# Graph layer and LayerNorm: one pass over column halves in eight banks, with A^T turned by VectorE

## The chip, the cores and the metric

One Trainium2 chip, one of its cores. The metric is the device time of one execution in microseconds. TensorE (PE) multiplies into PSUM, VectorE (DVE) and ScalarE (ACT) do the elementwise work, GpSimd (POOL) a little, and SyncE (SP) issues every DMA. PSUM has eight banks of 128 x 512 float32, and a matmul here fills one bank's width.

## What is computed

With x of 2048 x 512 and A = `adj` of 2048 x 2048, both float32:

```python
S = (A + A.T) * 0.5 + I
deg = S.sum(axis=1); dinv = deg ** -0.5            # 0 where deg <= 0
y = A @ (dinv[:, None] * S * dinv[None, :])        # Coefficient2 is adj, too
y = y @ x
out = layernorm(x + y)                             # over the 512 columns
```

Both kernels compute it as two products: U = dinv * (S @ (dinv * x)) and then A @ U. A matmul here takes the operand that is held in the array ("weights") transposed, so product 2 needs tiles of A^T in SBUF, and product 1 uses that S is symmetric. Each float32 operand is split into a high part (rounded to `float32r`) and a low part (what is left), and each product of two tiles is three matmuls: high with high, high with low, low with high.

## The kernel before

The matrices are cut into 16 blocks of 128 rows (N = 2048, NB = 16).

*Transposes.* Strip j is rows 128j to 128j+127 of A (`strip_row`, ring of 4), and `strip_col` holds the column block j below the diagonal. `transpose_batch` turns them on TensorE, 128 x 128 at a time, four to a batch, into banks 6 and 7; ACT copies each batch into `AT` (L342, `copy_batch`). There are 136 such transposes of row strips and 120 of column blocks, 256 in all.

*Degrees.* `row_sums` (DVE, L457) adds A^T's strip to A's strip in place and sums along the row; `sums_to_degrees`, `degree_root` (ACT, L356), `invert_root` (DVE, L493) and `degree` give dinv of the strip.

*Product 1.* The 16 row blocks of U are made in three groups of 6, 5 and 5 banks (`GROUPS`), and each group runs over all 16 strips k. For group 0, MH and ML are the high and low part of the first 768 columns of M = A + A^T in the strip (ACT L377, DVE L442) and ZH and ZL those of dinv * x (ACT L346, DVE L447). The strips' transposes run between group 0's products. Groups 1 and 2 load 640 columns of each strip again into `natural`, add A^T (L521), and split again. The "+ I" of S is worked in by `ex_scale` on POOL and `finish_u` on DVE (L515), which also release the banks between the groups.

*Product 2.* For each of the 16 output blocks m and each half h of the contraction (8 blocks), `half_high` (ACT, L412) and `half_low` (DVE, L539) split 128 x 1024 of `AT` into ATH and ATL, double-buffered; `column` runs 24 matmuls on each half. `layer_norm` follows a block behind.

Engines take their instructions in program order and wait on semaphores. `contract` on TensorE starts a step when both low parts are there:

```python
pe.wait_ge(ml_done, s + 1)
pe.wait_ge(zl_done, s + 1)
```

Of the kernel before, what the change touches and what calls it, by code (L numbers as in the profile page):

```python
# [5 lines left out]
P = 128  # L26
# [6 lines left out]
DEG_MIN = 1e-34  # L33
RING_R = 4
BATCH = 4
PIECES = 4


def gnn_resnorm_kernel(nc: bass.Bass, x: bass.AP, adj: bass.AP, out: bass.AP):
    N, D = x.shape  # L40
    NB = N // P
    GROUPS = [range(0, 6), range(6, 11), range(11, 16)]
    assert N == 2048 and D == 512 and GROUPS[-1][-1] == NB - 1
    GW = len(GROUPS[0]) * P
    G1 = len(GROUPS[1])
    UX_STEP = NB // 2
    HALF = NB // 2

    def batches(j):
        rows = [("row", c, min(BATCH, NB - c)) for c in range(j, NB, BATCH)]
        cols = [("col", r, min(BATCH, NB - r)) for r in range(j + 1, NB, BATCH)]
        return rows + cols

    BATCHES = [batches(j) for j in range(NB)]
    BATCH_BASE = [sum(len(b) for b in BATCHES[:j]) for j in range(NB + 1)]


    STRIPS = [[2], [3], [4, 5]] + [[j + 3] if j + 3 < NB else [] for j in range(3, NB)]  # L60
# [3 lines left out]
    AHEAD = 4  # L64
    FIRST_ROUND = [0, 0, 0, 2, 2]

    COPIES_FOR_SUM = [4, 2, 4, 3, 0]
    COPIES_FOR_D = [1, 2, 0, 2, 2, 0]

    def between_products(j):  # L70
        return [(i, n) for i in STRIPS[j] for n in range(len(BATCHES[i]))] 

    with ExitStack() as ctx:


        top = [(nc.sbuf_base + 31) // 32 * 32]
# [4 lines left out]
        def sb(name, shape, dt):  # L81
            size = 4
            for n in shape:
                size *= n
            top[0] += (size + 31) // 32 * 32
            return at(name, shape, dt, top[0] - (size + 31) // 32 * 32)

        AT = sb("AT", [NB, N], F32)
        uh_at = top[0]
        UH = sb("UH", [NB, D], F32R)  # L90
        ul_at = top[0]
        UL = sb("UL", [NB, D], F32R)
        strip_row = at("strip_row", [RING_R, N], F32, uh_at)
        ux = at("ux", [NB, D], F32, ul_at)
        strip_col = at("strip_col", [2, NB - 1, P], F32, ul_at + 8 * D * 4)

        slots_at = top[0]
        SLOT = 2 * D + 2 * GW
        sb("slots", [2, SLOT], F32)

        def in_slot(name, shape, dt, skip):
            return [at(f"{name}{i}", shape, dt, slots_at + (i * SLOT + skip) * 4) for i in range(2)]

        ZH = in_slot("ZH", [D], F32R, 0)
        ZL = in_slot("ZL", [D], F32R, D)
        MH = in_slot("MH", [GW], F32R, 2 * D)
        ML = in_slot("ML", [GW], F32R, 2 * D + GW)
        ATH = in_slot("ATH", [HALF, P], F32R, 0)
        ATL = in_slot("ATL", [HALF, P], F32R, HALF * P)

        xr = sb("xr", [2, D], F32)
        outr = sb("outr", [2, D], F32)
        natural = [at("natural0", [G1 * P], F32, top[0] - 2 * D * 4),
                   at("natural1", [G1 * P], F32, uh_at + 13 * D * 4)]
        ident = sb("ident", [P], F32)

# [27 lines left out]

        piece_in = [sem(f"piece_in{i}") for i in range(2 * PIECES)]
        row_in = [sem(f"row_in{i}") for i in range(RING_R)]
        col_in = [sem(f"col_in{i}") for i in range(2)]
        nat_in = [sem(f"nat_in{i}") for i in range(2)]
        x_in = [sem(f"x_in{i}") for i in range(2)]
        ux_in = [sem(f"ux_in{i}") for i in range(3)]  # L150
# [4 lines left out]
        msum_done = sem("msum_done")  # L155
        partial_done = sem("partial_done")
        PIECEWISE = 4
        PARTS = [sum(sum(kind == "col" for kind, _, _ in b) for b in BATCHES[:j]) for j in range(PIECEWISE + 1)]
        deg_done = sem("deg_done")
        newton_chain = sem("newton_chain")  # L160
        half_ready = sem("half_ready")
        degc_ready = sem("degc_ready")
        root_done = sem("root_done")
        inv_done = sem("inv_done")
        dinv_ready = sem("dinv_ready")
        mh_done = sem("mh_done")
        ml_done = sem("ml_done")
# [3 lines left out]
        ex_done = sem("ex_done")  # L171
        u_done = sem("u_done")
# [11 lines left out]
        LAST1 = 3 * NB  # L184

        def row_nth(j):
            return 16 * (j // RING_R + (j % RING_R > 0))

        def col_nth(j):
            return 16 * ((j + 1) // 2)  # L190

        def nth(s, slot):
            return 8 * s + (16 - 8 * slot)

        WIDTHS = [len(g) for g in GROUPS]
# [8 lines left out]
        def degree(j, engine, scaled):
            c = slice(j, j + 1)
            engine.wait_ge(inv_done, j + 1)
            scaled(corr[:, c], inv[:, c], deg_neg[:, c], 0.0).then_inc(newton_chain, 1)
            engine.wait_ge(newton_chain, 3 * j + 1)  # L210
            scaled(corr2[:, c], corr[:, c], inv[:, c], 1.5).then_inc(newton_chain, 1)
            engine.wait_ge(newton_chain, 3 * j + 2)
            scaled(dinv_open[:, c], corr2[:, c], inv[:, c], 0.0).then_inc(newton_chain, 1)
            engine.wait_ge(newton_chain, 3 * j + 3)
            scaled(dinv[:, c], dinv_open[:, c], mask[:, c], 0.0).then_inc(dinv_ready, 1)
            engine.wait_ge(dinv_ready, j + 1)
            scaled(dinv_half[:, c], dinv[:, c], 0.5, 0.0).then_inc(half_ready, 1)
# [8 lines left out]
        def _(sp):  # L226
            def load_x(k, s, slot):
                sp.dma_start(xr[:, slot, :], block(x, k)).then_inc(x_in[slot], 16)  # L228

            def load_ux(g, blocks):  # L230
                for m in blocks:
                    sp.dma_start(ux[:, m, :], block(x, m)).then_inc(ux_in[g], 16)  # L232

            def load_rows(j):
                if j >= RING_R:
                    sp.wait_ge(ml_done, j - RING_R + 1)
                if j == 0:
                    for n in range(PIECES):
                        cols = slice(n * N // PIECES, (n + 1) * N // PIECES)
                        sp.dma_start(strip_row[:, 0, cols], block(adj, 0)[:, cols]).then_inc(piece_in[n], 16)  # L240
                else:
                    sp.dma_start(strip_row[:, j % RING_R, :], block(adj, j)).then_inc(row_in[j % RING_R], 16)

            def load_cols(j):
                if j >= 2:
                    sp.wait_ge(tr_copied, BATCH_BASE[j - 1])
                size = BATCH if j == 0 else NB
                for n, r in enumerate(range(j + 1, NB, size)):
                    last = min(r + size, NB)
                    sp.dma_start(strip_col[:, j % 2, r - j - 1:last - j - 1, :],  # L250
                                 adj[r * P:last * P, j * P:(j + 1) * P].rearrange("(r p) c -> p r c", p=P)
                                 ).then_inc(col_in[j % 2] if j else piece_in[PIECES + n], 16)

            for j in range(RING_R):
                load_rows(j)
                if j < 3:
                    load_cols(j)
                if j < 2:
                    load_x(j, j, j)
            load_rows(RING_R)  # L260
            load_cols(3)
            for j in range(2, NB):
                if 2 < j < NB - 2:
                    load_rows(j + 2)
                sp.wait_ge(zl_done, j - 1)
                load_x(j, j, j % 2)
                if 1 < j and j + 2 < NB - 1:
                    load_cols(j + 2)
# [421 lines left out]
```

## Time and profile before

| | |
|---|---|
| time, median of 3 runs (lowest, highest) | 414.69 us (414.6, 416.33) |
| span of the profiled execution | 413.7 us |
| PE busy, share of span, instructions | 390.5 us, 94%, 1792 |
| DVE busy | 255.9 us, 62% |
| ACT busy | 166.6 us, 40% |
| DMA | 60.47 MB, mean 146 GB/s |
| first product matmul starts | 21.79 us |
| product 2 starts; last matmul starts | 233.20 us; 407.22 us |

The span runs from the first to the last instruction of one profiled execution. The timed runs lie about 1.0 us above it. A matmul's busy time in the trace overlaps its neighbours', so its pace is read from the starts of consecutive matmuls.

### The profile page before, as it was taken

The numbers are of one execution on the slowest core, as the hardware profiler recorded it, in microseconds if no ns is written. First come the engines' busy times: TensorE is split into PE (matmuls) and PEld (weight loads), VectorE is DVE, ScalarE is ACT, GpSimd is POOL, SyncE is SP. The second block draws the span as 40 slices with busy tenths as digits, with TensorE's granted clock in tenths as the row PEclk, the third lists the DMA queues.
The fourth block names the chain that finished last, engine by engine and source line by source line (L and its number), as shares of the span: only waits on it lengthen the run. The fifth ranks groups of instructions, "written<-read, shape, count | busy, mean of one in ns | idle before, by whom it ended". The sixth has DMA issues, their size and how long they took to land.

```text
span 413.7 us, 5648 instructions
## 1 busy us (share of the span) xinstructions
PE 390.5 (94%) x1792; PEld 318.8 (77%) x1792; DVE 255.9 (62%) x499; ACT 166.6 (40%) x309; POOL 50.5 (12%) x38
## 2 busy tenths in 40 slices
PE   5899999999988999979999999999999999999994
PEld 4677788777766888858888888888888888888883
DVE  0496877888798666897666654444455555554442
ACT  4666788676653444443344522222211222222210
POOL 0000000430079000094000430000000000000000
PEclk9999999999999999989999999999999999999998
DMA  7997988974474656766667001111111111111111
GB/s 229 353 345 242 361 272 278 398 291 155 117 248 131 178 176 173 206 199 165 175 175 189 26 2 51 52 51 51 51 51 51 51 51 51 48 35 42 28 49 51
DMA packets 36829, 60.47 MB, mean 146 GB/s; under 512 B 2640, under 2 KB 18000, under 8 KB 34896
## 3 DMA queue, kind: packets, MB, share of 16 engines
q1 hardware_dynamic: 36816, 60.30, 46.2%
q8 instruction: 7, 0.11, 0.1%
q14 instruction: 6, 0.05, 0.0%
HBM read 56.10 MB, written 4.19 MB: 146 GB/s over the span
## 4 chain that ended last, share of the span: by engine, by line
PE 78%; DVE 9%; DMA 5%; SPq 3%; ACT 2%; issue 2%; DVEq 0%; ACTq 0%
PE bank L609 25%; PE bank L611 24%; PE bank L610 24%; PE bank L605 5%; DMA strip_row<-in_adj 4%; DVE strip_row L457 2%; DVE ML L442 2%; DVE ZL L447 1%; DVE ux L515 1%; ACT AT L342 1%; SPq L232 1%; DMA natural<-in_adj 1%; ACT ZH L346 1%; SPq L228 1%; SPq L250 1%
## 5 line engine op out<-in xcount | busy, mean ns | idle before, releaser
L609 PE MATMUL bank<-ZL,MH 128*128 128x512 f32 x256 | 105.0, 410 | 7.9 <-DVE ML L442 6.1
L611 PE MATMUL bank<-ZH,MH 128*128 128x512 f32 x256 | 100.7, 393 | 0.0
L610 PE MATMUL bank<-ZH,ML 128*128 128x512 f32 x256 | 100.4, 392 | 0.0
L609 PE MATMUL bank<-UL,ATH 128*128 128x512 f32 x256 | 99.7, 389 | 0.0
L610 PE MATMUL bank<-UH,ATL 128*128 128x512 f32 x256 | 99.6, 389 | 0.0
L611 PE MATMUL bank<-UH,ATH 128*128 128x512 f32 x256 | 99.6, 389 | 0.0
L539 DVE TENSOR_TENSOR ATL<-AT,ATH 128x1024 fp32r<-128x1024 f32 x32 | 40.3, 1259 | 77.7 <-ACT ATH L412 77.7
L412 ACT ACTIVATE ATH<-AT 128x1024 fp32r (+1 forms) x32 | 34.0, 1061 | 84.1 <-PE bank L611 84.1
L609 PEld LDWEIGHTS bank<-ZL,MH 128*128 128x128 f32 x256 | 48.5, 190 | 19.5 <-DVE ML L442 9.1
L346 ACT ACTIVATE ZH<-xr,dinv 128x512 fp32r<-128x512 f32 x48 | 34.5, 719 | 59.4 <-DMA xr<-in_x 30.2
L611 PEld LDWEIGHTS bank<-ZH,MH 128*128 128x128 f32 x256 | 48.3, 189 | 10.4
L609 PEld LDWEIGHTS bank<-UL,ATH 128*128 128x128 f32 x256 | 48.0, 188 | 10.3 <-DVE ATL L539 0.3
L611 PEld LDWEIGHTS bank<-UH,ATH 128*128 128x128 f32 x256 | 48.1, 188 | 10.1
L610 PEld LDWEIGHTS bank<-UH,ATL 128*128 128x128 f32 x256 | 48.1, 188 | 9.8
L610 PEld LDWEIGHTS bank<-ZH,ML 128*128 128x128 f32 x256 | 48.7, 190 | 8.3
L447 DVE SCALAR_TENSOR_TENSOR ZL<-xr,dinv,ZH 128x512 fp32r<-128x512 f32 x48 | 40.3, 839 | 21.7 <-ACT ZH L346 21.6
L457 DVE SCALAR_TENSOR_TENSOR strip_row<-strip_row,AT 128x2048 f32<-128x2048 f32 (+8 forms) x27 | 38.1, 1431 | 19.6 <-ACT AT L342 19.6
L342 ACT ACTIVATE AT<-bank 128x512 f32<-128x512 f32 (+3 forms) x76 | 38.8, 527 | 27.6 <-PE bank L605 27.5
L326 POOL TENSOR_TENSOR UL<-ux,UH 128x512 fp32r<-128x512 f32 x16 | 25.6, 1631 | 113.5 <-ACT UH L352 113.5
L316 POOL TENSOR_SCALAR ux<-ux,dinv 128x512 f32<-128x512 f32 x16 | 24.2, 1530 | 76.2 <-DMA ux<-in_x 76.2
L521 DVE TENSOR_TENSOR natural<-natural,AT 128x640 f32<-128x640 f32 x32 | 27.1, 846 | 8.8 <-DMA natural<-in_adj 8.4
L605 PE MATMUL bank<-ident,strip_row 128*128 128x128 f32 x136 | 23.8, 309 | 7.6 <-DMA strip_row<-in_adj 6.9
(46 smaller groups left out, 250.8 us busy)
## 6 DMA issues: line engine op xcount, KB each, us to landing
xr<-in_x SPq DMA_DIRECT2D x64, 256.0 KB, 3.5
strip_row<-in_adj SPq DMA_DIRECT2D x15, 1024.0 KB, 7.3
natural<-in_adj SPq DMA_DIRECT2D x32, 320.0 KB, 3.4
ux<-in_x SPq DMA_DIRECT2D x16, 256.0 KB, 5.1
out<-outr SPq DMA_DIRECT2D x16, 256.0 KB, 2.0
strip_row<-in_adj SPq DMA_DIRECT2D x4, 256.0 KB, 4.3
strip_col<-in_adj SPq DMA_DIRECT2D x4, 256.0 KB, 6.8
strip_col<-in_adj SPq DMA_DIRECT2D x1, 896.0 KB, 9.6
```

What stands on the lines that cost most here:

```text
L326: nc.gpsimd.tensor_tensor(UL[:, m, :], ux[:, m, :], UH[:, m, :].bitcast(F32), ALU.subtract).then_inc(ul_done, 1)
L342: nc.scalar.activation(dst, src, ACT.Copy).then_inc(tr_copied, 1)
L346: nc.scalar.activation(ZH[slot][:, :], xr[:, slot, :], ACT.Copy, scale=dinv[:, bass.ds(k, 1)]).then_inc(zh_done, 1)
L412: nc.scalar.activation(ATH[h][:, :, :], AT[:, h * HALF:(h + 1) * HALF, bass.ts(m, P)], ACT.Copy).then_inc(ath_done, 1)
L447: nc.vector.scalar_tensor_tensor(out=ZL[slot][:, :], in0=xr[:, slot, :], scalar=dinv[:, bass.ds(k, 1)], in1=ZH[slot][:, :].bitcast(F32), o ...
L457: return nc.vector.scalar_tensor_tensor(out=strip[:, cols], in0=strip[:, cols], scalar=1.0, in1=AT[:, j, cols], op0=ALU.mult, op1=ALU.add, ...
L521: nc.vector.tensor_tensor(natural[slot][:, :], natural[slot][:, :], AT[:, bass.ds(k, 1), m0 * P:(m0 + G1) * P].rearrange("p o c -> p (o c) ...
L539: nc.vector.tensor_tensor(ATL[h][:, :, :], AT[:, h * HALF:(h + 1) * HALF, bass.ts(m, P)], ATH[h][:, :, :].bitcast(F32), ALU.subtract).then ...
L605: last = nc.tensor.transpose(TB[b % 2][:, i * P:(i + 1) * P], src, ident[:, :])
L609: nc.tensor.matmul(bank, wh, ml, start=start, stop=False)
L610: nc.tensor.matmul(bank, wl, mh, start=False, stop=False)
L611: return nc.tensor.matmul(bank, wh, mh, start=False, stop=stop)
```

## The change

The kernel is written anew around the same mathematics.

- `AT` is filled without TensorE for 14 of the 16 tiles. SP loads the columns of A straight into place as 32-row pieces (`load_block`, 4 DMAs per group of tiles, each into 32 partitions) so that only each 32 x 32 block is still to be turned; VectorE does that in place in one instruction for each tile (`turn`). Only tiles 0 and 1 are turned by TensorE, 32 transposes in place of 256.
- Tiles from 4 on are interleaved four by four (tiles 2 and 3 two by two): tile t of a group takes every fourth row and column. The weights of a matmul are then read with a step of 4 elements (`own_columns`, `half_weights`), as are the rows that `turned_rows` gives to VectorE.
- Product 1 runs over halves of the columns, eight banks at once: 32 steps (`STEPS`) of 8 x 3 matmuls. Steps 0 to 3 are half 0 of tiles 0 to 3; ACT saves the banks into `part`. Steps 4 to 19 are half 1 of all 16 tiles. Steps 20 to 31 are half 0 of tiles 4 to 15, with 1024 columns of each strip loaded again (`hstrip`). There are 32 x 24 = 768 matmuls, as before (48 steps of 5 or 6 x 3).
- "+ I" becomes 2I added to the diagonal block of the strip (`add_diagonal`); POOL's `ex_scale` and DVE's `finish_u` are gone. POOL does dinv's small chain.
- Product 2 takes half 1 of blocks 0 to 2 first, then their half 0, then block by block, in eight banks in turn.

Core of the diff:

```diff
-    GROUPS = [range(0, 6), range(6, 11), range(11, 16)]
+    GROUPS = [(0, 1), (1, 1), (2, 2), (4, 4), (8, 4), (12, 4)]
+    BY_PE = 2
+    EARLY = 4
+    STEPS = [(t, 0) for t in range(EARLY)] + [(t, 1) for t in range(NB)] + [(t, 0) for t in range(EARLY, NB)]
...
+            def load_block(first, quads):
+                size = dict(GROUPS)[first]
+                for a in quads:
+                    c0 = first * P + Q * size * a
+                    dst = group_area(first)[Q * a:Q * (a + 1)].rearrange("p (b e) -> p b e", b=N // Q)
+                    src = adj[:, c0:c0 + Q * size].rearrange("(b r) c -> r b c", r=Q)
+                    sp.dma_start(dst, src).then_inc(block_in[first], 16)
+            def load_strip(t):
+                if t >= EARLY:
+                    sp.wait_ge(sl_done, t + 1)
+                sp.dma_start(strip[t % 4][:, :], own_rows(adj, t)).then_inc(strip_in[t % 4], 16)
...
+            load_block(4, range(4))
+            load_xg(4)
+            load_strip(4)
+            load_strip(5)
+            load_block(8, range(4))
+            load_strip(6)
+            load_xg(8)
+            load_strip(7)
+            sp.wait_ge(prod_done, 8 * (S_BETA + EARLY))
+            load_strip(8)
+            load_block(12, range(0, 2))
+            load_strip(9)
+            load_block(12, range(2, 4))
+            load_strip(10)
...
+            for s in range(S_BETA, S_END):        # ACT
+                t, _ = STEPS[s]
+                s_high(s)
...
+                if 2 * EARLY <= s + 1 < S_END:
+                    z_high(z_index(s + 1))
+                if s < S_GAMMA and EARLY <= t + 3 < NB:
+                    degree_root(t + 3)
...
+            def turn(t):
+                first, _ = GROUP_OF[t]
+                dve.wait_ge(block_in[first], 64)
+                v = turned_rows(t, 0, N).rearrange("p (b r) -> p b r", r=Q)
+                nc.vector.transpose(v, v).then_inc(turned, 1)
...
+            for s in range(S_BETA, S_END):        # DVE
+                t, _ = STEPS[s]
+                s_low(s)
...
+                if s < S_GAMMA and EARLY <= t + 2 < NB:
+                    invert_root(t + 2)
+                if 2 * EARLY <= s + 1 < S_END:
+                    z_low(z_index(s + 1))
+                if s < S_GAMMA and t + 4 < NB:
+                    turn(t + 4)
+                if s < S_GAMMA and EARLY <= t + 3 < NB:
+                    sum_rows(t + 3)
+                    sums_to_degrees(t + 3)
+                    if t + 3 >= 8:
+                        add_diagonal(t + 3, strip_half(t + 3))
+                if S_GAMMA <= s + 2 < S_END:
+                    half_rows(s + 2)
```

**VectorE in product 1.** Before, one strip of group 0 (j at or past 4) was this on VectorE: the sum of the next strip, four small instructions of its degree, then the low parts of this strip.

```order
L457 SCALAR_TENSOR_TENSOR strip_row,rowsum<-strip_row,AT 128x2048
L482 TENSOR_SCALAR deg<-rowsum 128x1
L484 TENSOR_SCALAR degc<-deg 128x1
L485 TENSOR_SCALAR deg_neg<-deg 128x1
L486 TENSOR_SCALAR mask<-deg 128x1
L442 TENSOR_TENSOR ML_62<-strip_row,MH_60 128x768
L447 SCALAR_TENSOR_TENSOR ZL_58<-xr,dinv,ZH_56 128x512
L493 RECIPROCAL inv<-root 128x1
```

Now one step of half 1 (here step 9, tile 5: low part of tile 5's strip, low part of x for step 10, `turn` of tile 9, sum of tile 8, then the next step's low part) is this, on the same engine:

```order
L517 TENSOR_TENSOR SL_76<-strip_54,SH_74 128x1024
L501 RECIPROCAL inv<-root 128x1
L524 SCALAR_TENSOR_TENSOR ZLr_83<-xg_58,dinv,ZHr_81 128x512
L461 STREAM_TRANSPOSE AT<-AT 128x2048
L464 SCALAR_TENSOR_TENSOR strip_53,rowsum<-strip_53,AT 128x2048
L487 TENSOR_SCALAR mask<-rowsum 128x1
L488 TENSOR_SCALAR deg_90<-rowsum 128x1
L493 TENSOR_TENSOR strip_53<-strip_53,twice 128x128
L517 TENSOR_TENSOR SL_75<-strip_55,SH_73 128x1024
```

The transpose is new there, the low part of the strip is 1024 columns wide in place of 768, and two of the small instructions of the degree are gone.

**ScalarE in the same steps**, the high part of step 9's strip (`SH`), the high part of x for step 10, the root of tile 8's degree, and the high part of step 10's strip:

```order
L362 ACTIVATE SH_74<-strip_54 128x1024
L376 ACTIVATE ZHr_81<-xg_58,dinv 128x512
L346 ACTIVATE root<-deg_90 128x1
L362 ACTIVATE SH_73<-strip_55 128x1024
```

The root stands ahead of the next step's high part; it waits for the degree that VectorE makes at the end of its list above, and VectorE's next low part waits for that high part.

**SyncE's DMA queue**, from the second strip on (`xg` are rows of x, `strip` are rows of A, `AT` the pieces of `load_block`):

```order
L222 DMA AT<-in_adj 32x64x64 x4
L227 DMA strip_55<-in_adj 128x2048
L234 DMA xg_57<-in_x 128x1024
L227 DMA strip_56<-in_adj 128x2048
L222 DMA AT<-in_adj 32x64x128 x4
L234 DMA xg_58<-in_x 128x2048
L227 DMA strip_53<-in_adj 128x2048
L227 DMA strip_54<-in_adj 128x2048
L222 DMA AT<-in_adj 32x64x128 x4
L227 DMA strip_55<-in_adj 128x2048
L234 DMA xg_57<-in_x 128x2048
L227 DMA strip_56<-in_adj 128x2048
```

Before, a strip's rows and its column block (at most 14 x 128 columns, into 128 partitions) alternated in this queue; now 4 MB of pieces for four tiles go in one go, and the strip of tile 6 stands behind the pieces of tiles 8 to 11.

## Rows read from the trace of the kernel before

**Rows 1.** The page: span, and busy time of each engine (share) xinstructions.
```profile
span 413.7 us, 5648 instructions
...
PE 390.5 (94%) x1792; PEld 318.8 (77%) x1792; DVE 255.9 (62%) x499; ACT 166.6 (40%) x309; POOL 50.5 (12%) x38
```

**Rows 2.** The page: shares of the chain that ended last, by engine.
```profile
PE 78%; DVE 9%; DMA 5%; SPq 3%; ACT 2%; issue 2%; DVEq 0%; ACTq 0%
```

**Rows 3.** Timeline of PE in product 2: start us, us, engine, line, operation.
```profile
233.20 0.39 PE L609 MATMUL bank<-UL,ATH 128*128 128x512 f32 x1
...
300.00 0.39 PE L609 MATMUL bank<-UL,ATH 128*128 128x512 f32 x1
...
300.68 0.39 PE L609 MATMUL bank<-UL,ATH 128*128 128x512 f32 x1
...
407.22 0.39 PE L611 MATMUL bank<-UH,ATH 128*128 128x512 f32 x1
```

**Rows 4.** Groups of PE instructions: count, busy us, mean ns, idle before.
```profile
L605 PE MATMUL bank<-ident,strip_row 128*128 128x128 f32 x136 | 23.8, 309 | 7.6 <-DMA strip_row<-in_adj 6.9 <-ACT AT L342 0.6
...
L605 PE MATMUL bank<-ident,strip_col 128*128 128x128 f32 x120 | 20.9, 307 | 1.5 <-ACT AT L342 1.3
```

**Rows 5.** Timeline of PE in product 1.
```profile
21.79 0.47 PE L609 MATMUL bank<-ZL,MH 128*128 128x512 f32 x1
...
62.15 0.48 PE L609 MATMUL bank<-ZL,MH 128*128 128x512 f32 x1
...
63.28 0.48 PE L609 MATMUL bank<-ZL,MH 128*128 128x512 f32 x1
```

**Rows 6.** Timeline of PE's weight loads in product 1.
```profile
62.12 0.19 PEld L609 LDWEIGHTS bank<-ZL,MH 128*128 128x128 f32 x1
62.23 0.19 PEld L610 LDWEIGHTS bank<-ZH,ML 128*128 128x128 f32 x1
```

**Rows 7.** Timeline of DVE at the start.
```profile
14.00 0.15 DVE L482 TENSOR_SCALAR deg<-rowsum 128x1 f32<-128x1 f32 x1
...
18.77 0.16 DVE L493 RECIPROCAL inv<-root 128x1 f32<-128x1 f32 x1 [4.31 <-ACT root L356]
```

**Rows 8.** Groups of DVE instructions, shapes apart.
```profile
L539 DVE TENSOR_TENSOR ATL<-AT,ATH 128x1024 fp32r<-128x1024 f32 x32 | 40.3, 1259 | 77.7 <-ACT ATH L412 77.7
...
L457 DVE SCALAR_TENSOR_TENSOR strip_row<-strip_row,AT 128x2048 f32<-128x2048 f32 x12 | 27.8, 2315 | 8.3 <-ACT AT L342 8.3
```

**Rows 9.** Timeline of DVE, one strip of product 1.
```profile
98.17 2.29 DVE L457 SCALAR_TENSOR_TENSOR strip_row<-strip_row,AT 128x2048 f32<-128x2048 f32 x1
...
100.51 0.15 DVE L482 TENSOR_SCALAR deg<-rowsum 128x1 f32<-128x1 f32 x1
...
101.75 0.75 DVE L447 SCALAR_TENSOR_TENSOR ZL<-xr,dinv,ZH 128x512 fp32r<-128x512 f32 x1
102.41 0.16 DVE L493 RECIPROCAL inv<-root 128x1 f32<-128x1 f32 x1
```

**Rows 10.** Groups of ACT instructions, shapes apart.
```profile
L346 ACT ACTIVATE ZH<-xr,dinv 128x512 fp32r<-128x512 f32 x48 | 34.5, 719 | 59.4 <-DMA xr<-in_x 30.2 <-PE bank L611 28.7 <-DVE dinv L489 0.5
...
L412 ACT ACTIVATE ATH<-AT 128x1024 fp32r x28 | 29.7, 1061 | 76.1 <-PE bank L611 76.1
```

**Rows 11.** DMA from 14 to 15 us, when only 512-byte packets were under way.
```profile
DMA packets 573, 0.29 MB, mean 293 GB/s; under 512 B 0, under 2 KB 573, under 8 KB 573
```

**Rows 12.** DMA from 73 to 76 us, packets of 2 and 8 KB.
```profile
DMA packets 564, 1.24 MB, mean 412 GB/s; under 512 B 63, under 2 KB 71, under 8 KB 529
```

**Rows 13.** DMA issues: count, KB each, median us to landing.
```profile
strip_col<-in_adj SPq DMA_DIRECT2D x1, 704.0 KB, 5.3
```

**Rows 14.** Timeline of PE at the change from group 1 to group 2.
```profile
180.49 0.50 PE L609 MATMUL bank<-ZL,MH 128*128 128x512 f32 x1 [2.44 <-DVE ML L442]
...
182.78 0.63 PE L609 MATMUL bank<-ZL,MH 128*128 128x512 f32 x1
183.21 0.63 PE L610 MATMUL bank<-ZH,ML 128*128 128x512 f32 x1
```

More of the change, by code:

```diff
@@ L60, in gnn_resnorm_kernel @@
[L60 to L71, printed above, removed]
+    assert N == 2048 and D == 512
+    HALF = N // 2
+    HB = NB // 2
+    GROUPS = [(0, 1), (1, 1), (2, 2), (4, 4), (8, 4), (12, 4)]
+    GROUP_OF = {t: (first, size) for first, size in GROUPS for t in range(first, first + size)}
@@ L206, in degree, with group_area @@
[L206 to L217, printed above, removed]
+        def group_area(t):
+            first, size = GROUP_OF[t]
+            return AT[:, first * N:(first + size) * N]
@@ L244, in load_cols @@
[L244 to L268, printed above, removed]
-                if j == UX_STEP:
-                    load_ux(0, GROUPS[0])
@@ L302, in _ @@
-            for slot in range(2):
-                store(NB - 2 + slot, slot)
+            def load_block(first, quads):
[5 more added lines that the diff above has]
+                    sp.dma_start(dst, src).then_inc(block_in[first], 16)
@@ L304, in _ @@
+            load_x_last(0)
+            load_x_last(1)
+            for m in range(NB):
+                sp.wait_ge(o_ready, m + 1)
+                sp.dma_start(block(out, m), outr[:, m % 2, :]).then_inc(out_done[m % 2], 16)
+                if m + 2 < NB:
+                    load_x_last(m + 2)
             for slot in range(2):
@@ L665, in _, with transpose_batch @@
-            pe.wait_ge(u_done, GROUPS[2][0] - 1)
-            column(0, 0, first=True)
-            column(1, 1)
-            with pe.Fori(1, NB // 2) as i:
-                for slot in range(2):
-                    pe.wait_ge(y_read, 2 * i + (slot - 1))
-                    column(2 * i + slot, slot)
+            def transpose_batch(b):
+                t, n = b // CHUNKS, b % CHUNKS
+                pe.wait_ge(colpiece_in[n] if t == 0 else col1_in, 16)
+                bank = banks[4 + n] if t == 0 else banks[6 + n % 2]
+                if t > 0:
+                    pe.wait_ge(tr_copied, b - 1)
+                for i in range(4):
+                    last = nc.tensor.transpose(bank[:, i * P:(i + 1) * P], col[t][:, n * 4 + i, :], ident[:, :])
+                last.then_inc(tr_done, 1)
```

868 lines of the change are left out of this document (466 added, 402 removed).

## The prediction

> **What bounds the kernel now.** I read the page first: TensorE is busy 94% of a span of 413.7 us [rows 1], and the chain that ended last is PE for 78%, DVE for 9%, DMA for 5% [rows 2]. So the matmul stream is the bound, with gaps. Its pace comes from starts in the timeline: three matmuls in 0.68 us, from 300.00 to 300.68, 0.2267 us each; 768 of them are 174.1 us, and product 2 does run without a gap from 233.20 to 407.22 + 0.23 [rows 3]. After that come 6.3 us for the last LayerNorm and store. Product 1 has 768 matmuls too, another 174.1 us, but takes from 21.79 [rows 5] to 233.20, 211.4 us. The difference, 37.3 us, has two parts. Between two equal points of a round with four transposes lie 1.13 us (62.15 to 63.28); less three matmuls, 0.45 us, 0.11 for a transpose [rows 5]. There are 256 transposes [rows 4]; 60 come before the first product, so 196 x 0.113 = 22.2 us lie in product 1, and 15.1 us are waits, mostly where groups change. So 413.7 = 21.8 + 348.2 + 22.2 + 15.2 + 6.3.
>
> **TensorE's part of the change.** Matmuls stay at 1536, 348.2 us. Of the transposes 16 stay inside product 1, 1.8 us: a gain of 20.4. The start gets shorter: 16 transposes before the first product in place of 60, and the first root no longer stands behind four copies of strip 1 on ACT, where it made DVE wait 4.3 us [rows 7]. The first row sum is ready at 11 us (it was at 14.0 [rows 7], with 31 transposes ahead); root, high part 1.06 and high part of x 0.72 [rows 10] follow, so the first product starts at 13.5, a gain of 8.3. If nothing else waited, the span would be 13.5 + 348.2 + 1.8 + 6.3 = 369.8. The question is what product 1 waits for. One step is 24 x 0.2267 = 5.44 us.
>
> **DVE's part.** I list a step of half 1 by distances between starts, since neighbouring instructions overlap by about 0.1 us. Low part of the strip, 1024 columns: 1.26 busy [rows 8], 1.17 as a distance. Reciprocal 0.12. Low part of x 0.66 (101.75 to 102.41) [rows 9]. Row sum over 2048 columns 2.34 (98.17 to 100.51) [rows 9]. Degree, first two instructions, 0.3. The turn of 128 x 2048 in place has no row. The nearest is the row sum, one pass over as many elements in 2.3 us [rows 8]; half of it, 1.1, if two elements pass at a time, and 4.4 if a turn needs two passes or its step of four elements costs. I take 2.2. Then comes a wait: the root (0.1) and the next high part (1.0) stand on ACT behind the degree, and DVE's next low part waits for them. Sum: 1.17 + 0.12 + 0.66 + 2.2 + 2.34 + 0.3 + 0.1 + 1.0 + some 0.1 of signalling = 8.0 us, against TensorE's 5.44. Steps 5 and 6 have no low part of x: 7.3. So from step 5 to 16 product 1 goes at DVE's pace, and TensorE idles 2.6 us in each step. This alone gives back some 28 us of the 29 saved.
>
> **The DMA part.** Blocks are packets of 512 bytes into 32 partitions. Such packets alone moved at 293 GB/s into 128 partitions [rows 11], the upper end. One load of 704 KB landed in 5.3 us [rows 13], 136 GB/s with its latency, the lower end. Between ends far apart I take about the middle, 220: 4.19 MB of four tiles take 19.1 us, the two tiles of 2 and 3 (256-byte packets, at the same rate) 9.5. Strips and x go at 412 GB/s [rows 12]: 2.5 us a strip. The Trainium skill, page "SBUF — State Buffer", section "Door 1: The DMA port swizzle", says that a transfer to 32 partitions reaches half of the ports and measures 189 GB/s against 328 for 128 partitions. No row here shows such a transfer; at 190 GB/s the sum below would be near 436, at that page's asymptote of 218 it would be as below.
>
> **The schedule.**
> - Tiles 1 to 3. The pieces, x, column 1 and strip 1 keep the queue busy to 15, and blocks 2 and 3 land at 26.6. Turn, sum, root, high and low part each lie one behind the other: step 1 starts at 25, step 2 at 34, step 3 at 41.5, step 4 at 47. TensorE alone would be at 37.
> - Block 4 starts in the queue at 31.4, takes 19.1 and lands at 52. Turn 4 comes first, so step 5's low part is done at 55.4; steps 6 and 7 start at 61.4 and 68.7.
> - Block 8 starts at 59.2 behind strips 4 and 5 and ends at 78.3; strip 6, behind it, lands at 82.4. Its sum, root, high part put step 8 at 86.2, where DVE alone would have put it at 76.7: 9.5 us more.
> - Eight steps at 8.0, and 2.5 us where strip 10 lies behind block 12: step 16 at 152.7.
> - Steps 16 to 31 are TensorE's again: 16 x 5.44 = 87.0, and some 5 us at the seam at step 20, where eight UH and UL must be made ahead of the banks, in DVE's and ACT's order. End of product 1: 244.8. The half rows of the last 12 steps (1.2 us), low parts (1.2 and 0.7) come to 3.3 us of DVE in 5.44 and lie under TensorE; so do their loads, 0.75 MB a step.
> - Product 2: 174.1, TensorE's, since a half needs 1.06 + 1.26 us of splitting [rows 8, 10] under 5.44. End 6.3.
> Sum 244.8 + 174.1 + 6.3 = 425.2 for the span; the runs' median of before is 1.0 over its span (414.69 to 413.7), so 426 us, slower by 2.7%. Before, product 1 had 15 us of waits; now 55.
>
> **Edits costed at nothing.** The 2I on the diagonal is 0.2 us of DVE in the 0.3 wait for ACT. POOL's small chain for dinv has a whole step of 8 us. Eight banks take away the two changes of groups, which is in the waits of before that I dropped. The clock: after the gaps at the change from group 1 to group 2, TensorE's matmuls came every 0.43 us in place of 0.23 for 3 us [rows 14], the lower of the two levels; two long waits here (steps 5 and 8) could cost 1 to 2 us each so.
>
> **Rivals.**
> 1. *Faster, or no change: blocks at the full rate.* If 32 partitions cost nothing, the block of four tiles takes 14.3 us at 293 GB/s [rows 11]. Then strip 6 is late by 5 less, blocks 4 and 12 hide behind DVE, and product 1 ends near 231 to 233: 412 to 414 us. With a turn of 1.1 us a step is 6.9: another 11 x 1.1 less early overlap, 404. Against it: with the waits above, nothing below 404 can come from the rows. It ends faster than before when a step of half 1 takes under about 7.9 us on average with no wait for a block. Chance 0.31 for the two, 0.2 of it clearly faster.
> 2. *Slower by much: the step of four elements.* Each matmul has its own weight load. Loads start 0.11 us apart at the closest [rows 6], and a matmul takes 0.2267, so a load may get twice as dear for nothing. From there it decides: three quarters of the matmuls (1152) read weights with the step, and each 0.01 us over 0.2267 costs 11.5 us; at 0.30 the time is near 510. On DVE, a turn of 4.4 us gives 442. No row reads with such a step. Chance 0.12. The skill's page of SBUF, same section, says that an access that finds fewer than two hits in a 16-byte line pays a penalty; four float32 elements are 16 bytes, so by it this rival would hold, unless the load, at half the pace of the moving operand, absorbs it. No run here shows it so far.
> 3. *The forecast:* DVE's pace and the blocks' rate together, 418 to 436. Chance 0.57.
>
> **How the numbers follow.** About 0.5% (2 us) can be told from no change. Faster: 0.2 of rival 1, and 0.07 for a schedule that overlaps more than my sum has it, as before: 0.27. Same: 0.13, the slow side of rival 1. Slower: 0.6, the forecast and rival 2. The range leaves out 0.06 below 404 and the worst of rival 2, about 0.12, above 442. The likeliest time is that of the forecast, 425 to 426.
>
> **What would show it.** PE's first product at 13 to 14 us; MATMUL starts 0.227 apart with the stepped weights; STREAM_TRANSPOSE near 2.2 us; starts of steps 9 to 16 near 8.0 apart, each third matmul waiting for `SL`, and DVE's `SL` for ACT's `SH` by 1.0 to 1.2; a wait of DVE for `strip` of tile 6 near 75 us and one of the first turn of tile 4 for its block; product 2 174 us. The forecast is wrong if blocks move at 290 GB/s or more, if the turn is far from 2.2, or if weight loads with a step slow the matmuls.

## The result and the profile after

The changed kernel is slower by 14.6%: 475.75 us in the median (473.47 to 477.74, 4 runs) against 414.97, a ratio of 1.1458 with a 95% interval of 1.141 to 1.1505. The forecast of "slower" was right, its size was not: 425 to 426 was forecast, and 475.75 lies above the range, which ended at 442. In this document medians and ratios leave out a run that lies over 1.5% above the fastest of its kernel.

First the page of the changed kernel's profile: span, busy time of the engines, and the granted clock of TensorE in 40 slices.

```profile
span 475.9 us, 4138 instructions
...
PE 404.4 (85%) x1568; PEld 364.3 (77%) x1568; DVE 300.7 (63%) x440; ACT 114.4 (24%) x190; POOL 30.1 (6%) x68
...
PEclk9988969858878887898999999999999999999998
```

Against [rows 1] TensorE has 224 instructions fewer and is busy longer, 404.4 us for 390.5, and VectorE is busy 45 us longer with fewer instructions. VectorE has new work, the 14 turns, but TensorE has none; instructions may have become slower, or the clock lower. The groups of VectorE's instructions, shapes apart (busy us, mean ns), say which:

```profile
L464 DVE SCALAR_TENSOR_TENSOR strip<-strip,AT 128x2048 f32<-128x2048 f32 x15 | 52.9, 3529 | 12.9 <-ACT AT L341 8.4 <-DMA strip<-in_adj 4.4
L461 DVE STREAM_TRANSPOSE AT<-AT 128x2048 f32<-128x2048 f32 x14 | 52.2, 3727 | 11.1 <-DMA AT<-in_adj 11.1
...
L533 DVE TENSOR_TENSOR hstrip<-hstrip,AT 128x1024 f32<-128x1024 f32 x12 | 24.1, 2012 | 0.0
```

The row sum over 2048 columns took 2315 ns before [rows 8] and takes 3529 in the mean. The sum of a half strip (`hstrip`, 1024 columns) takes 2.0 us where 1.2 was forecast. Both read A^T through `turned_rows`. VectorE's timeline at step 8 shows single ones:

```profile
101.66 1.23 DVE L517 TENSOR_TENSOR SL<-strip,SH 128x1024 fp32r<-128x1024 f32 x1 [1.22 <-ACT SH L362]
102.80 0.16 DVE L501 RECIPROCAL inv<-root 128x1 f32<-128x1 f32 x1
102.88 0.73 DVE L524 SCALAR_TENSOR_TENSOR ZLr<-xg,dinv,ZHr 128x512 fp32r<-128x512 f32 x1
103.53 3.96 DVE L461 STREAM_TRANSPOSE AT<-AT 128x2048 f32<-128x2048 f32 x1
107.38 3.81 DVE L464 SCALAR_TENSOR_TENSOR strip<-strip,AT 128x2048 f32<-128x2048 f32 x1
...
111.23 0.15 DVE L487 TENSOR_SCALAR mask<-rowsum 128x1 f32<-128x1 f32 x1
...
112.66 1.23 DVE L517 TENSOR_TENSOR SL<-strip,SH 128x1024 fp32r<-128x1024 f32 x1 [1.22 <-ACT SH L362]
```

Read by distances of starts, one step is 1.14 + 0.08 + 0.65 + 3.85 (turn) + 3.85 (sum) + 1.43 (degree, ScalarE's root and high part) = 11.0 us; the forecast had 8.0. TensorE waits for this loop in every step from 8 to 15, as its own timeline says at steps 8 and 9:

```profile
101.68 0.82 PE L691 MATMUL bank<-ZHr,SH 128*128 128x512 f32 x1 [7.72 <-ACT SH L362]
...
112.68 0.62 PE L691 MATMUL bank<-ZHr,SH 128*128 128x512 f32 x1 [2.48 <-ACT SH L362]
```

Product 2, which no other engine holds up, is slower too. Its first and last matmul, and below them three weight loads of it:

```profile
289.28 0.40 PE L727 MATMUL bank<-UH,ATH 128*128 128x512 f32 x1
...
469.46 0.40 PE L729 MATMUL bank<-UH,ATL 128*128 128x512 f32 x1
```

```profile
299.87 0.31 PEld L729 LDWEIGHTS bank<-UH,ATL 128*128 128x128 f32 x1
300.10 0.31 PEld L727 LDWEIGHTS bank<-UH,ATH 128*128 128x128 f32 x1
300.34 0.31 PEld L728 LDWEIGHTS bank<-UL,ATH 128*128 128x128 f32 x1
```

767 distances in 180.2 us are 0.235 us a matmul, against 0.2267 [rows 3]; these loads take 0.31 us where they took 0.19 [rows 6]. Last, the DMA from 48 to 58 us, when blocks of tiles 4 to 7 were nearly all that was under way:

```profile
DMA packets 3676, 2.07 MB, mean 207 GB/s; under 512 B 31, under 2 KB 3650, under 8 KB 3650
```

### The profile page after: what moved, and what is told of

Same layout as the page of the kernel before. It is cut to its first block, busy times and chain, and to the rows that moved or that the text cites. A ratio compares the mean times of both kernels' runs of the same rounds, so it can differ in the third digit from the quotient of the medians.

```text
span 475.9 us, 4138 instructions
## 1 busy us (share of the span) xinstructions
PE 404.4 (85%) x1568; PEld 364.3 (77%) x1568; DVE 300.7 (63%) x440; ACT 114.4 (24%) x190; POOL 30.1 (6%) x68
## 4 chain that ended last, share of the span: by engine, by line
PE 55%; DVE 25%; SPq 9%; DMA 7%; ACT 3%; issue 2%; ACTq 0%; DVEq 0%
PE bank L727 12%; PE bank L728 12%; PE bank L729 12%; DVE AT L461 9%; DVE strip L464 8%; PE bank L697 6%; PE bank L691 6%; PE bank L694 6%; SPq L222 6%; DMA AT<-in_adj 4%; DMA strip<-in_adj 3%; ACT SH L362 2%; SPq L227 2%; DVE SL L517 2%; DVE ZLr L524 1%
## 5 line engine op out<-in xcount | busy, mean ns | idle before, releaser
L691 PE MATMUL bank<-ZHr,SH 128*128 128x512 f32 x192 | 85.6, 446 | 34.0 <-ACT SH L362 29.2
L610 DVE TENSOR_TENSOR ATL<-AT,ATH 128x256 fp32r<-128x256 f32 (+2 forms) x64 | 41.5, 690 | 82.8 <-ACT ATH L402 82.8
L691 PEld LDWEIGHTS bank<-ZHr,SH 128*128 128x128 f32 x192 | 54.4, 284 | 41.8 <-ACT SH L362 32.0
L697 PE MATMUL bank<-ZHr,SL 128*128 128x512 f32 x192 | 84.5, 440 | 1.9 <-DVE SL L517 1.8
L694 PE MATMUL bank<-ZLr,SH 128*128 128x512 f32 x192 | 82.9, 432 | 0.0
L464 DVE SCALAR_TENSOR_TENSOR strip<-strip,AT 128x2048 f32<-128x2048 f32 (+1 forms) x19 | 55.7, 2932 | 23.1 <-ACT AT L341 12.9
L697 PEld LDWEIGHTS bank<-ZHr,SL 128*128 128x128 f32 x192 | 54.3, 283 | 11.0 <-DVE SL L517 6.4
L461 DVE STREAM_TRANSPOSE AT<-AT 128x2048 f32<-128x2048 f32 x14 | 52.2, 3727 | 11.1 <-DMA AT<-in_adj 11.1
L402 ACT ACTIVATE ATH<-AT 128x256 fp32r<-128x256 f32 (+2 forms) x64 | 36.9, 624 | 89.3 <-PE bank L729 85.5
L694 PEld LDWEIGHTS bank<-ZLr,SH 128*128 128x128 f32 x192 | 54.6, 284 | 4.3
## 6 DMA issues: line engine op xcount, KB each, us to landing
AT<-in_adj SPq DMA_DIRECT2D x12, 1024.0 KB, 15.7
```

Of the source, the lines that this page charges most:

```text
L402: ins = nc.scalar.activation(half_place(ATH[i % 2], lo, hi), src, ACT.Copy)
L461: nc.vector.transpose(v, v).then_inc(turned, 1)
L464: return nc.vector.scalar_tensor_tensor(out=strip[t % 4][:, cols], in0=strip[t % 4][:, cols], scalar=1.0, in1=turned_rows(t, cols.start, c ...
L610: ins = nc.vector.tensor_tensor(half_place(ATL[i % 2], lo, hi), src, half_place(ATH[i % 2], lo, hi).bitcast(F32), ALU.subtract)
L691: nc.tensor.matmul(banks[b][:, :], wh, zh[:, :], start=first, stop=False)
L694: nc.tensor.matmul(banks[b][:, :], wh, zl[:, :], start=False, stop=False)
```

## The experiments

Times are medians; ratios are to the kernel before, timed on the same chip, and the brackets are their 95% intervals. Two words in one: a read with a "step of four" takes every fourth element of a row, while "step 8" is one of the 32 steps of product 1. "Dense" kernels read neighbouring elements where the changed kernel reads every fourth (or second), and "wide" loads bring the same bytes to other places; both do the same amount of work on other numbers than the layer's, so they measure a cost and do not replace the kernel.

**1. VectorE's reads of A^T dense** (`dve_dense`).

```diff
 def turned_rows(t, c0, c1):
-    first, size = GROUP_OF[t]
-    return group_area(t).rearrange("p (i k) -> p k i", k=size)[:, t - first, c0:c1]
+    return AT[:, t * N + c0:t * N + c1]
```

> VectorE reads and turns the tile's 2048 elements of AT one after the other instead of with a step of four; loads, matmuls and all counts stay (the numbers of U are then others). Theory A (the step of four costs VectorE): turns fall from 3.95 to 2.3 us and row sums from 3.8 to 2.3, a step of half 1 from 11.0 to about 8 us, the time by 25 to 35 us, to 441 to 450. Theory B (the block loads at 207 GB/s set the pace of product 1): the turns get shorter but wait for blocks and strips, and the time falls by less than 12 us. Theory C (TensorE at half its clock): the step stays above 10 us whatever VectorE does.

447.73 us, ratio 1.0781 [1.0734, 1.0827]: 28 us less, theory A. Where nothing waits for a load a step of half 1 now takes 7.7 to 8.7 us, so theory C is out. The groups of VectorE in it:

```profile
L463 DVE SCALAR_TENSOR_TENSOR strip<-strip,AT 128x2048 f32<-128x2048 f32 x15 | 34.0, 2265 | 23.3 <-DMA strip<-in_adj 15.8 <-ACT AT L340 7.4
L460 DVE STREAM_TRANSPOSE AT<-AT 128x2048 f32<-128x2048 f32 x14 | 32.2, 2303 | 13.9 <-DMA AT<-in_adj 13.9
```

The busy time of the two falls by 38.9 us (from 105.1 to 66.2), of which 28 reach the time; the waits of these two groups for loads grow by 14 us, from 11.1 and 4.4 to 13.9 and 15.8. So theory B holds a part: the loads are next in line.

**2. TensorE's weights dense** (`pe_dense`).

```diff
-wh, wl = own_columns(SH[s % 2], m, half), own_columns(SL[s % 2], m, half)
+wh, wl = SH[s % 2][:, b * P:(b + 1) * P], SL[s % 2][:, b * P:(b + 1) * P]
...
-    return buf[:, lo:lo + size * P].rearrange("p (i k) -> p k i", k=size)[:, k - first, :]
+    return buf[:, (k % 8) * P:(k % 8 + 1) * P]
```

> Only the weights of the matmuls are read densely (128 neighbouring columns), all else as changed. Theory A (the matmul's pace of 0.2345 us in place of 0.2267 comes from weight loads with a step of four, 0.31 us in place of 0.19): product 2 falls from 180.4 to 174.2 us, product 1 little, since VectorE sets it, 6 to 9 us in all: 467 to 470. Theory B (the 0.2345 has another cause, as the order of the three matmuls or the banks): no change.

466.29 us, ratio 1.1237 [1.1201, 1.1273]: 9.5 us less, theory A. Its weight loads in product 2 last as long as before, and the matmuls are 0.2276 us apart (767 distances in 174.6 us):

```profile
299.85 0.19 PEld L728 LDWEIGHTS bank<-UH,ATL 128*128 128x128 f32 x1
300.07 0.19 PEld L726 LDWEIGHTS bank<-UH,ATH 128*128 128x128 f32 x1
300.30 0.19 PEld L727 LDWEIGHTS bank<-UL,ATH 128*128 128x128 f32 x1
```

**3. Both** (`all_dense`).

> Both of the above together: every read with a step of four made dense, the loads unchanged. If the two add up: 434 to 443. What is left over the kernel before (415) is then the price of the block loads and of the wait for ScalarE's high part in each step. If the step of four were all of the loss, it would come to 415 or below.

442.02 us, ratio 1.0668 [1.0604, 1.0733]: 33.7 us less than the changed kernel, against 28.0 + 9.5 one by one. The step of four is the larger part of the loss, not all of it. Here step 12 starts at 132.76 and step 16 at 164.65, 8.0 us a step: the forecast's loop, once its reads are dense. What the loads do in this kernel is seen in VectorE's timeline:

```profile
60.38 2.31 DVE L459 STREAM_TRANSPOSE AT<-AT 128x2048 f32<-128x2048 f32 x1 [12.48 <-DMA AT<-in_adj]
...
93.21 2.29 DVE L462 SCALAR_TENSOR_TENSOR strip<-strip,AT 128x2048 f32<-128x2048 f32 x1 [12.21 <-DMA strip<-in_adj]
```

The first turn of tile 4 waits for its block, and the sum of tile 6 for the strip behind block 8, as forecast; they come at 60.4 and 93.2 where 52 and 82.4 were forecast.

**4. ScalarE's root behind the next high part** (`root_later`; computes the layer in full).

```diff
 s_high(s)
+if s <= S_GAMMA and EARLY <= t + 2 < NB and STEPS[s - 1] == (t - 1, 1):
+    degree_root(t + 2)
...
-if s < S_GAMMA and EARLY <= t + 3 < NB:
-    degree_root(t + 3)
```

> The changed kernel, with ScalarE's root of the degree of tile t+3 moved behind the next step's high part instead of ahead of it, so that VectorE needs not wait for it. Theory A (the 1.2 us of VectorE's wait for SH in each of 12 steps is on the path): 12 to 15 us less, 461 to 464. Theory B (the time is only moved to another wait, as for blocks): within 4 us of 475.

465.1 us, ratio 1.1199 [1.1137, 1.126]: 10.7 us less, somewhat under theory A's 12 to 15. VectorE's wait for SH, 16.5 us in all in the changed kernel, is 2.4 here.

**5. Blocks into 128 partitions** (`wide_loads`).

```diff
-dst = group_area(first)[Q * a:Q * (a + 1)].rearrange("p (b e) -> p b e", b=N // Q)
-src = adj[:, c0:c0 + Q * size].rearrange("(b r) c -> r b c", r=Q)
+dst = group_area(first)[:, a * w:(a + 1) * w].rearrange("p (b e) -> p b e", b=NB)
+src = adj[:, c0:c0 + Q * size].rearrange("(b r) c -> r b c", r=P)
```

> The changed kernel, with each quarter of a block loaded into 128 partitions instead of 32: the same bytes in the same 512-byte (tiles 2 and 3: 256-byte) packets, so A^T's contents are others. Theory A (207 GB/s comes from the 32 partitions): the rate of the blocks rises to about 290 GB/s, the waits of 11 us for the first turn of tile 4 and of 4 us for strip 6 go, and 7 to 12 us come off 475.8. Theory B (512-byte packets are slow in themselves, or the source's rows are): still near 207 GB/s and no change.

462.71 us, ratio 1.1116 [1.1078, 1.1154]: 13.0 us less, a little over theory A. From 36 to 48 us, in the block of tiles 4 to 7, DMA moves 295 GB/s, a quarter of a block lands 11.0 us after its issue in place of 15.7, and neither the first turn of tile 4 nor the sum of tile 6 waits for a load any more.

**6, 7. The causes taken away together** (`dense_wide`, `dense_wide_root`).

> Wide loads and all reads dense. With VectorE at 8 us a step the loads weigh more: theory A takes 17 to 25 us off the 442 of all_dense, to 417 to 425, my forecast's rival with loads at full rate (412 to 414) plus the waits it missed at the start. Theory B: 440 or more.

> As dense_wide, and ScalarE's root behind the next high part. If the three costs (step of four, 32 partitions, the wait for ScalarE) are all of it, 8 to 12 us less than dense_wide and at or under the kernel before: 405 to 415.

422.31 us, ratio 1.0164 [1.013, 1.0199], and 415.43 us, ratio 1.0001 [0.9978, 1.0023]. From the changed kernel down: 475.75, minus 33.7 (step of four) is 442.0, minus 19.7 (32 partitions) is 422.3, minus 6.9 (the wait for ScalarE, where 8 to 12 was expected) is 415.4. The shares depend on the order: taken away alone, the three gave 33.7, 13.0 and 10.7. With all three gone the new order of work is worth the old one, within the interval. TensorE's 20 us of transposes and the 6 us of start that the change saves (first product at 15.7 us for 21.8) are still given back, by this kernel's trace to VectorE's loop of 6.8 us a step and to the first tiles.

**8, 9. Interleaved two by two** (`pairs`, `pairs_root`; both compute the layer in full). Every read has a step of two at most, the packets of blocks are 256 bytes, and SyncE's queue is ordered anew: blocks of two tiles, one of them with its rows of x now ahead of strip 5, one ahead of strip 7.

```diff
-    GROUPS = [(0, 1), (1, 1), (2, 2), (4, 4), (8, 4), (12, 4)]
+    GROUPS = [(0, 1), (1, 1)] + [(t, 2) for t in range(2, 16, 2)]
```

> The changed kernel with tiles interleaved two by two from tile 2 on, so that every read has a step of two elements (8 bytes) and the packets of the blocks are 256 bytes. Theory A (a step of two costs VectorE nothing, as the turns of tiles 2 and 3 with 2.3 us show, and the smaller packets cost DMA more): turns and sums 2.3 us, matmuls 0.227 apart, but blocks at 140 to 170 GB/s, so product 1 is set by loads, some 9.5 us a tile: 445 to 465. If loads do not bound it, 435 to 442 as all_dense.

> pairs (steps of two elements, 256-byte packets) with the root behind the next high part. VectorE's step is then near 6.8 us, and the loads of a tile, near 9.5 us, set the pace of product 1: less than 4 us off 458.5. If VectorE set it, 10 us or more.

457.23 us, ratio 1.0985 [1.0902, 1.1067]; 450.07 us, ratio 1.0889 [1.0836, 1.0942]. A step of two is free for VectorE (its turns take 2.30 us) but not for TensorE: product 2 runs from 270.12 to 448.98 + 0.23 us, 0.233 a matmul, where 0.227 was expected. Its weight loads take 0.19 us, as long as dense ones. `pairs` is still some 15 us above `all_dense`. Product 2 has 4 of them, and VectorE's row sums wait 27.4 us for strips, against 4.4 in the changed kernel. The rate is not the reason, and the expected 140 to 170 GB/s missed: from 41 to 50 us `pairs` moves 213 GB/s and the changed kernel 205. The new order of the queue is the nearest candidate, but no run tried it apart. The root's move gave 7.2 us by the medians and 4 by the ratios, whose intervals overlap: a gain of 10 or more, with VectorE alone setting the pace, is not seen, but this does not say whether it is under 4.

**10. What a step costs** (`steps`, a bench: it times single instructions and does not compute the layer).

> A bench, not the layer (out is not computed; it holds leftovers): VectorE sums of 128x2048 with one input read with a step of 1, 2, 3, 4 and 8 elements, sums written with a step of 1, 2, 4, turns in place with a step of 1 to 4 and one read with a step of 4 and written densely; ScalarE copies with a step of 1, 2, 4, 8; 24 matmuls each with weights read with a step of 1, 2, 3, 4, 8. Theory A (a read pays as soon as each element lies in another 16 bytes, a write does not): sums 2.2 us at steps 1 to 3, 3.8 at 4 and 8; turns 2.3 and 3.95, also with dense output; written sums 2.2 throughout. Theory B (the price grows with the distance): step 3 lies between, step 8 above step 4. For the weight loads 0.19 us at 1 to 3 and 0.31 at 4 and 8 under A.

VectorE's timeline, one row for each kind (each ran twice): sums with one input read with a step of 1, 2, 3, 4, 8; sums written with a step of 2 and 4; turns in place with a step of 2, 3, 4; a turn read with a step of 4 and written densely.

```profile
46.09 2.29 DVE L60 TENSOR_TENSOR res<-dense,big 128x2048 f32<-128x2048 f32 x1 [19.61 <-ACT acts L78]
...
50.75 2.29 DVE L60 TENSOR_TENSOR res<-dense,big 128x2048 f32<-128x2048 f32 x1
...
55.41 2.91 DVE L60 TENSOR_TENSOR res<-dense,big 128x2048 f32<-128x2048 f32 x1
...
61.24 3.79 DVE L60 TENSOR_TENSOR res<-dense,big 128x2048 f32<-128x2048 f32 x1
...
68.88 3.85 DVE L60 TENSOR_TENSOR res<-dense,big 128x2048 f32<-128x2048 f32 x1
...
81.29 2.29 DVE L62 TENSOR_TENSOR wide<-dense 128x2048 f32<-128x2048 f32 x1
...
85.94 3.79 DVE L62 TENSOR_TENSOR wide<-dense 128x2048 f32<-128x2048 f32 x1
...
98.28 2.31 DVE L65 STREAM_TRANSPOSE big<-big 128x2048 f32<-128x2048 f32 x1
...
102.98 2.88 DVE L65 STREAM_TRANSPOSE big<-big 128x2048 f32<-128x2048 f32 x1
...
108.80 3.94 DVE L65 STREAM_TRANSPOSE big<-big 128x2048 f32<-128x2048 f32 x1
...
116.73 3.79 DVE L68 STREAM_TRANSPOSE res<-big 128x2048 f32<-128x2048 f32 x1
```

Nothing at 2, a quarter more at 3, 65% more at 4, and hardly more at 8. Both theories missed a part: step 3 is not free, and a write with a step of 4 costs as much as a read. This fits a price on the share of elements that begin another 16 bytes: half at step 2, three quarters at 3, all from 4 on. The Trainium skill, page "SBUF — State Buffer", section "Door 1: The DMA port swizzle", has this as a rule of two hits in each 16-byte line, and VectorE's rows agree. ScalarE pays more (1.92 us dense, 3.91 at step 4), though in the changed kernel it reads no row with a step:

```profile
29.80 1.92 ACT L78 ACTIVATE acts<-big 128x2048 f32<-128x2048 f32 x1
...
33.82 3.91 ACT L78 ACTIVATE acts<-big 128x2048 f32<-128x2048 f32 x1
```

TensorE's weight loads at steps 2, 3, 4 and 8:

```profile
38.00 0.19 PEld L85 LDWEIGHTS bank<-mov,wts 128*128 128x128 f32 x1
...
42.93 0.25 PEld L85 LDWEIGHTS bank<-mov,wts 128*128 128x128 f32 x1
...
47.63 0.31 PEld L85 LDWEIGHTS bank<-mov,wts 128*128 128x128 f32 x1
...
53.38 0.33 PEld L85 LDWEIGHTS bank<-mov,wts 128*128 128x128 f32 x1
```

Here too step 3 is dearer than expected. The matmuls of the four groups start 0.233, 0.2355, 0.235 and 0.245 us apart (21 distances each). The dense group, most of which ran at the lower clock, ends at 0.229, and the kernel before has 0.227. So most of what a step of four costs TensorE, some 0.006 of 0.008 us, is there at a step of two already, where the load is no longer than a dense one. The length of the load alone is thus not what sets the pace; what does stays open.

**11. What 32 partitions cost** (`loads`, a bench).

> A bench, not the layer: 4 MB of A in 512-byte packets, six ways one after the other. Phase 0: four DMAs into 32 partitions each, in order 0, 1, 2, 3 (as load_block). Phase 1: order 0, 2, 1, 3. Phase 2: sixteen DMAs, alternating between partitions 0 to 63 and 64 to 127. Phase 3: 128 partitions each. Phase 4: quarters 0, 1 from SyncE and 2, 3 from ScalarE at the same time. Phase 5: 2048-byte packets into 32 partitions each. Theory A (32 partitions share half of the ways into SBUF): phases 0 and 1 near 207 GB/s, phase 3 near 290, phase 4 above 207 if the two queues' transfers truly overlap, phase 5 near 215. Theory B (the packets or the 256 KB between rows read by an engine are the cause): phase 5 near 400 and phase 3 near 207.

DMA in the middle of each of the six phases (columns: stretch, its length, POOL busy, clock, DMA share, GB/s):

```profile
3.00:20.00 17.00, 0.00 (x0) 1.00 1.21 208
26.00:40.00 14.00, 0.00 (x0) 1.00 1.20 209
47.00:63.00 16.00, 0.00 (x0) 1.00 1.21 210
69.00:82.00 13.00, 0.00 (x0) 1.00 1.17 295
86.00:98.00 12.00, 0.00 (x0) 1.00 1.18 283
104.00:120.00 16.00, 0.00 (x0) 1.00 1.07 209
```

Theory A in each phase. From one queue, 32 partitions for each transfer give 208 to 210 GB/s whatever the order, the alternation or the packet (512 or 2048 bytes); 128 partitions give 295; and two queues that write different halves at once give 283.

**12. Two queues in the kernel** (`queues` on `root_later`, `pairs_queues` on `pairs_root`; both compute the layer in full): ScalarE issues quarters 2 and 3 of each block.

```diff
+for first in {6: [8], 9: [12]}.get(s, ()):
+    load_block(nc.scalar, first, range(2, 4))
```

> root_later, with quarters 0 and 1 of each block issued by SyncE and quarters 2 and 3 by ScalarE, so that both halves of the partitions are written at a time. Output and data as in the reference. Theory A (two queues lift the blocks from 207 to near 290 GB/s in the kernel, as in phase 4 of the bench): 8 to 14 us less than root_later's 465.5, as wide_loads gave 13. Theory B (in the kernel the strips between the blocks keep them apart, or ScalarE is held up while it issues): 3 us or less, or slower.

> pairs_root with the same split over two queues. Here loads weigh most (256-byte packets into 32 partitions). Theory A: blocks faster and product 1 at VectorE's 6.8 us a step, 12 to 25 us less than 451, 426 to 439. Theory B: 256-byte packets have a fixed price for each of the 16 engines, so that the 32 partitions are not their limit: within 5 us of 451.

463.34 us, ratio 1.1158 [1.1106, 1.121], and 453.77 us, ratio 1.0915 [1.0866, 1.0965]: by the medians 1.8 us less and 3.7 us more than without, neither clear of noise, since the intervals overlap. The rate did rise in `queues`; from 40 to 46 us it is

```profile
DMA packets 3434, 1.74 MB, mean 290 GB/s; under 512 B 32, under 2 KB 3434, under 8 KB 3434
```

where `root_later` has 204 GB/s. But ScalarE pays for it. Its timeline, with its own issuing (ACTq):

```profile
66.55 11.42 ACTq L219 DMA_DIRECT2D AT<-in_adj  x2
78.02 1.06 ACT L363 ACTIVATE SH<-strip 128x1024 fp32r<-128x1024 f32 x1 [11.27 <-issue]
```

It is held for 11.4 us while it issues two transfers of 1 MB behind others that are still under way, and the high part of step 7 starts only then. Theory A is right on the rate, theory B on the time. `pairs_queues` is within 5 us too, as its theory B has it; its reason, a fixed price for each packet, was not shown.

**13. Strip 6 ahead of half a block** (`root_split` on `root_later`; computes the layer in full).

```diff
-load_block(8, range(4))
+load_block(8, range(0, 2))
 load_strip(6)
+load_block(8, range(2, 4))
```

> root_later with strip 6 put between the halves of block 8 in the queue. Theory A (VectorE's wait for strip 6 behind the whole block is on the path): 4 to 7 us less than root_later's 465.5. Theory B (the pace of the loads through this stretch decides, whichever comes first): within 2 us.

465.27 us, ratio 1.1185 [1.1122, 1.1248], the same as `root_later`: theory B. The strip landed at 86 us instead of 95 and the block at 98 instead of 92.

## Why the prediction was right and wrong

Compared with the forecast's schedule (span 425.2, measured 475.9), step 8 starts at 101.7, forecast 86.2 (+15.5); the eight steps to step 16 take 88.3 us, forecast 66.5 (+21.8); from there to the end of product 1 99.3, forecast 92.1 (+7.2); product 2 180.4, forecast 174.1 (+6.3). `all_dense`, the same kernel with its reads dense, divides this miss. Its last three stretches take 67.6, 92.8 and 174.8 us, within 1.2 of the forecast, and its step 8 starts at 97.0, 10.8 late. So the reads with a step are behind nearly all that was missed from step 8 on; what is left lies ahead of step 8, where the loads come late.

- **What bounds it: right.** VectorE's loop sets half 1 of product 1, and blocks delay the first turn of tile 4 (11.1 us) and the sum of tile 6 (4.4 us), at the places named.
- **DVE's part: the step that failed.** The row sum was taken at 2.34 us from a row of dense reads and given no bound, though it reads the same `turned_rows` as the turn; it is 3.85. The turn was chosen at 2.2 between 1.1 and 4.4; it is 3.85 as a distance where tiles are interleaved by four, and 2.3 for tiles 2 and 3. Together the two are 3.2 us more in each step, 11.0 in place of 8.0. Run 1 shows that VectorE's reads are worth 28 us, and run 10 that the step of four is the price, for a read and a write alike.
- **TensorE's part.** 0.2267 was carried over; with a step of four it is 0.235, and run 2 shows 9.5 us. Rival 2 had the place right, but held that a load might get twice as dear for nothing. With loads of 0.31 us for 0.19 the matmul is 0.008 us dearer: neither free nor the 0.30 that was priced. By runs 8 and 10 the load's length alone is not the mechanism, since some 0.006 of it come at a step of two with loads of 0.19 us. The rival's price of 442 for VectorE's share counted the turn alone, and the range ended there; the measured time lies between its prices of 442 and 510.
- **The rule of two hits in a 16-byte line** (the Trainium skill, page "SBUF — State Buffer", section "Door 1: The DMA port swizzle") stood beside rival 2, whose chance was put at 0.12. VectorE's rows agree with it: 3.79 us for 2.29 at a step of four, and no price at two.
- **The DMA part: the rate right, the queue too early.** 220 was taken and 207 GB/s measured (at the blocks of four), though as a middle of two far ends, so with some luck. The Trainium skill, page "SBUF — State Buffer", section "Door 1: The DMA port swizzle", has 189 measured and 218 as the asymptote for 32 partitions, and the trace lies between. Runs 5 and 11 show that the partitions are the cause; taken away, they are worth 13 us alone and 20 us with VectorE unburdened, more than the 12 to 14 by which rival 1 lies under the forecast. The time was missed by the queue. What stands ahead of the blocks of tiles 2 and 3 landed at 20.1 us (15 forecast), these blocks at 31.4 (26.6), and strip 3, ahead of block 4, at 39.3 (31.4), so that block 4 came at 61.7 where 52 was forecast:

```profile
61.72 3.94 DVE L461 STREAM_TRANSPOSE AT<-AT 128x2048 f32<-128x2048 f32 x1 [11.06 <-DMA AT<-in_adj]
```

- **The wait for ScalarE: right** as a place and a size (1.2 us a step); worth 10.7 us, of the 12 to 15 expected of run 4.
- **The schedule's start: too early.** The first product was at 15.59 us, not 13.5, and step 4 at 53.76, not 47 (51.9 in `all_dense`). Step 0 began with matmuls 0.43 us apart (17.74 and 18.16 below), the pace of the lower level of the clock [rows 14]. The transposes of tile 1 stand between these matmuls, so that strip 1's sum began only at 25.08 us, behind the last of ScalarE's copies, and step 1 at 31.2, where 25 was forecast. How much of this the clock alone cost was not tried apart.

```profile
17.74 0.63 PE L691 MATMUL bank<-ZHs,SH 128*128 128x512 f32 x1
18.16 0.63 PE L694 MATMUL bank<-ZLs,SH 128*128 128x512 f32 x1
```

- **The clock: underrated.** Two waits were priced at 1 to 2 us each. About 120 matmuls of the changed kernel start 0.38 to 0.5 us after the one ahead, in the first microseconds after a wait; from 101.7 to 190 us the granted clock was 0.80 in the mean. About 23 us of TensorE's time go there. How much of it reaches the end was not tried apart, but most lies in steps that then wait anyway: at step 9 TensorE still waited 2.48 us, though step 8 had begun at the lower level.
- **A small slip of the sum:** the forecast puts a run's time 1.0 us above its span. In the runs of the record it lies 1.8 above the span of the same run.

## What to carry to other kernels

A changed access pattern reprices every instruction that reads through it, the old ones included: list all its readers before a row of a dense read is carried over. For float32 on VectorE keep the step at two elements, or give the layout's cost to the engine that has time. When a first use of loaded data is forecast, follow the queue from its first byte, since what is late there stays late. When work moves from a busy engine to an idle one, add up the new loop through all engines: even at 6.8 us a step (run 7), against TensorE's 5.4, the gain was gone.

## What the runs showed of the hardware

A step of 4 elements (16 bytes) costs VectorE 65% (3.79 for 2.29 us), on reads and writes alike and not twice for both (an in-place turn 3.94), and ScalarE 104% (3.91 for 1.92). A step of 3 costs VectorE 27%, a step of 2 nothing. A weight load takes 0.19, 0.25, 0.31 and 0.33 us at steps of 2, 3, 4 and 8, and matmuls of 512 columns then follow each other after 0.233, 0.2355, 0.235 and 0.245 us, against 0.227 with dense weights. One queue's transfers into 32 partitions run at 208 to 210 GB/s in the three orders tried, but two queues, writing partitions 0 to 63 and 64 to 127 at the same time, reach 283 to 290. The Trainium skill, page "SBUF — State Buffer", section "Can I just issue two DMAs to hit both halves?", says that two concurrent ones gain 6%; within one queue the runs agree, across two queues they do not, and the measurement decides. An engine that issues DMAs behind many others under way can be held: ScalarE was for 11.4 us by two of 1 MB (run 12), and SyncE for 21.4 us by the four of block 4 in the changed kernel.
